# A recurrent and FP4 feed-forward layer on one core: stacking the short Down slice, splitting the pointwise product, moving layernorm sums and reordering the first chunk

## The reference

```
xn = layernorm(x)
# branch s: causal conv -> recurrence -> MLP, each with an RMS norm and a residual
x1 = pointwise(causal_dwconv3(rmsnorm(xn))) + xn
x2 = scan(sigmoid(gate), g(hidden)) + x1        # gate, hidden = rmsnorm(x1) @ gru_w.T
s  = gelu(rmsnorm(x2) @ w1.T + b1) @ w2.T + b2 + x2
# branch g: a SwiGLU whose operands are rounded to FP4 in blocks of 16
h  = silu(fp4(xn) @ fp4(w_gate).T) * (fp4(xn) @ fp4(w_up).T)      # 704 wide
g  = silu(fp4(h) @ fp4(w_down).T)
out = x + s * g
```

## Time and profile before

| | us |
|---|---|
| median of 3 runs (1084.41 to 1086.84) | 1085.59 |
| the profiled execution | 1085.26 |
| its span, first to last instruction | 1083.5 |
| PE busy in the span | 1061.8 (98%) |
| DVE busy | 934.5 (86%) |
| ACT busy | 607.3 (56%) |
| POOL busy | 147.5 (14%) |

### The profile page before, as it was taken

How to read it: one execution, slowest core, us unless ns; L and a number is a source line. 1 busy time by engine, 2 the same in 40 slices (tenths; PEclk the granted TensorE clock), 3 DMA queues, 4 the chain that set the end, 5 groups by cost and what they waited for, 6 DMA issues and landing times. The chain is left out here.

```text
span 1083.5 us, 18319 instructions
## 1 busy us (share of the span) xinstructions
PE 1061.8 (98%) x6954; PEld 967.9 (89%) x6954; DVE 934.5 (86%) x1720; ACT 607.3 (56%) x967; POOL 147.5 (14%) x123
## 2 busy tenths in 40 slices
PE   7899999999999999999999999999999999999998
PEld 6788989989898998989999898998989899898998
DVE  6978988989888898988889898898989889898895
ACT  5564464564746547474654747455574645647452
POOL 1230101112020110201111010111101011120010
PEclk9999999999999999999999999999999999999999
DMA  7000001010010101001010010101001010100110
GB/s 248 1 21 1 1 2 59 1 60 1 1 59 1 59 1 47 13 2 59 1 60 1 21 40 1 59 1 60 1 1 59 1 59 1 59 1 2 39 40 21
DMA packets 29365, 31.45 MB, mean 29 GB/s; under 512 B 1120, under 2 KB 28512, under 8 KB 29280
## 3 DMA queue, kind: packets, MB, share of 16 engines
q1 hardware_dynamic: 28448, 29.43, 8.7%
q10 hardware_dynamic: 832, 0.87, 0.2%
HBM read 21.90 MB, written 8.39 MB: 28 GB/s over the span
## 5 line engine op out<-in xcount | busy, mean ns | idle before, releaser
L990 PE MATMUL gu_ps<-gu_hi,xq_hi 128*128 128x352 f32 x512 | 168.3, 329 | 0.0
L990 PE MATMUL gu_ps<-gu_lo,xq_hi 128*128 128x352 f32 x512 | 165.9, 324 | 0.0
L990 PE MATMUL gu_ps<-gu_hi,xq_lo 128*128 128x352 f32 x512 | 165.7, 324 | 0.0
L990 PE MATMUL w_ps<-w_hi,act_hi 128*128 128x256 f32 x480 | 140.1, 292 | 0.0
L990 PE MATMUL w_ps<-w_hi,act_lo 128*128 128x256 f32 x480 | 135.1, 281 | 0.0
L990 PE MATMUL w_ps<-w_lo,act_hi 128*128 128x256 f32 x480 | 134.9, 281 | 0.0
L990 PE MATMUL w_ps<-dn_hi,hqt_hi 128*128 128x256 f32 x384 | 116.6, 304 | 2.0 <-DVE hqt_lo L519 2.0
L990 PE MATMUL w_ps<-dn_hi,hqt_lo 128*128 128x256 f32 x384 | 108.5, 283 | 0.0
L990 PE MATMUL w_ps<-dn_lo,hqt_hi 128*128 128x256 f32 x384 | 108.4, 282 | 0.0
L818 ACT ACTIVATE g<-w_ps 128x256 f32<-128x256 f32 x64 | 24.7, 385 | 147.7 <-PE w_ps L990 147.6
L496 DVE TENSOR_TENSOR hid<-sl,gu_ps 128x704 f32<-128x704 f32 x64 | 56.8, 887 | 58.8 <-PE gu_ps L990 58.2
(11 more groups left out here) (136 smaller groups left out, 2703.6 us busy)
## 6 DMA issues: line engine op xcount, KB each, us to landing
x_in<-x_dram SPq DMA_DIRECT2D x16, 512.0 KB, 5.8
x_res<-x_dram SPq DMA_DIRECT2D x16, 512.0 KB, 5.0
out_dram<-o SPq DMA_DIRECT2D x15, 512.0 KB, 3.5
act<-w_t_dram SPq DMA_DIRECT2D x1, 1024.0 KB, 11.3
w_f<-w_t_dram SPq DMA_DIRECT2D x1, 1024.0 KB, 13.8
w_f<-w_down_dram SPq DMA_DIRECT2D x1, 704.0 KB, 9.4
hid<-w_gate_dram SPq DMA_DIRECT2D x1, 640.0 KB, 5.9
hid<-w_up_dram SPq DMA_DIRECT2D x1, 640.0 KB, 9.3
```

The source lines that it names most:

```text
L990: done = M.matmul(psum, l, r, start=first and i == 0, stop=last and i == len(terms) - 1)
```

## The change

- Down: `fp4_hidden_values` writes the last 64 quantised features twice, so the sixth slice holds them in rows 0 to 63 and again in rows 64 to 127 (the memset is gone). `hidden_low` makes low parts for five slices in one subtraction and, in a second small one, replaces rows 64 to 127 of the sixth high slice by their low part. `down` then needs 5 x 3 + 2 = 17 matmuls for a tile.
- Pointwise: `pw` and `y` are split in high and low parts. PE does three fp32r matmuls in place of each fp32 product (12 in place of 8 instructions for a chunk); ACT gets `front_y_high`, DVE `front_y_low`. `y_hi` and `y_lo` share their memory with `keep` and `cand`.
- Layernorm sums: `front_moments` is cut in two. `front_stats(c+2)` is the last DVE step of `body(c)`, and the rest (aggregation) moves into the next body between `hidden_values(c-1,2)` and the second group of `gelus_low`. SP issues each `load` ahead of the `store` beside it.
- `gelus_low` is cut as `range(4)` and `range(4, 8)` in place of `range(5)` and `range(5, 8)`. `output_sum` is as before.
- Small moves in `body`: `output(c-1,1)` ahead of `scaled_low(2c+1)`, `front_xc(c+1)` ahead of all of `ff1(c)`, `front_y` behind the first gelu, the taps ahead of the last quantisation step.
- `first()`: the low parts of `w1` and `w2` are made on DVE (`ff_low`) and no longer on POOL, and the weight steps 3 to 5 go between the tiles of `ff1(0)`; some `keep_busy` counts change; `pointwise(1)` is last.

The core of the diff:

```diff
             with sp.Fori(0, B - 3) as i:
+                load(i + 3)
                 store(i)
-                load(i + 3)
...
             def first():
                 layernorm_scales(0, 1)
-                low_weights(0)
+                gru_low()
                 rms_scale(0)
-                pool.wait_ge(xslo_ready, KD)
-                low_weights(1)
                 rms_scale(1)
-                pool.wait_ge(xslo_ready, 2 * KD)
-                low_weights(2)
                 layernorm_scales(1, 3)
...
+            def fp4_hidden_values(dst, rounded):
+
+                n, last = NBI * FP4_BLOCK, NFULL * P // FP4_BLOCK
+                fp4_values(dst[:, 0:n], NBI, rounded)
+                return V.scalar_tensor_tensor(blocks(dst[:, n:KI * P], NBI - last),
+                                              blocks(q_m[:, NFULL * P:n].bitcast(BF16), NBI - last),
+                                              1.0 / UNIT, spread(q_scale[:, last:NBI], NBI - last),
+                                              ALU.mult, ALU.mult)
...
-                V.tensor_tensor(hqt_lo[:], hqt_ps, hqt_hi[:].bitcast(F32), ALU.subtract).then_inc(hqtlo_ready, 1)
+                V.tensor_tensor(hqt_lo[:], hqt_ps[:, 0:NFULL, :], hqt_hi[:, 0:NFULL, :].bitcast(F32), ALU.subtract)
+
+                twin = hqt_hi[LAST:P, NFULL, :]
+                V.tensor_tensor(twin, hqt_ps[LAST:P, NFULL, :], twin.bitcast(F32),
+                                ALU.subtract).then_inc(hqtlo_ready, 1)
...
             def body(c, front):
                 hidden_values(c - 1, 1, fp4_round(NBI, carried["ratios"]))
-                gelus_low(c - 1, range(5))
+                gelus_low(c - 1, range(4))
                 hidden(c, 0)
...
                 hidden_values(c - 1, 2, fp4_round(NBI, ratios))
-                gelus_low(c - 1, range(5, KF))
+                if front and c > 1:
+                    front_moments(carried["stats"])
+                gelus_low(c - 1, range(4, KF))
                 hidden(c, 2)
...
-                if front:
-                    front_moments(c + 1)
+                if front and c == 1:
+                    front_moments(front_stats(c + 1))
                 recurrence(c, 0)
...
+                output(c - 1, 1, w_ps[:, 1, :])
                 scaled_low(c * 2 + 1)
-                output(c - 1, 1, w_ps[:, 1, :])
...
                 if front:
-                    front_fp4_values(c + 1, front_fp4_ratios(c + 1))
+                    ratios = front_fp4_ratios(c + 1)
                     front_taps(c + 1)
+                    front_fp4_values(c + 1, fp4_round(T * NBD, ratios))
+                    front_y_low(c + 1)
                     carried["ratios"] = fp4_ratios(hid[:, 1, :], NBI, hidden_scales(c, 1))
                     hidden_low(c, 0)
                     front_fp4_low(c + 1)
+                    if c + 2 < B:
+                        carried["stats"] = front_stats(c + 2)
...
-                        last = product(w_ps[:, e, :], pw[:, k, e * P:(e + 1) * P], y[:, k, :], False, k == KD - 1)
+                        last = product(w_ps[:, e, :], (pw_hi[:, k, e * P:(e + 1) * P], pw_lo[:, k, e * P:(e + 1) * P]),
+                                       (y_hi[:, k, :], y_lo[:, k, :]), False, k == KD - 1)
...
-                for k in range(KI):
-                    last = product(bank[:, 0:D], (hqt_hi[:, k, :], hqt_lo[:, k, :]),
-                                   (dn_hi[:, k, :], dn_lo[:, k, :]), k == 0, k == KI - 1)
-                last.then_inc(dn_done, 1)
+                for k in range(NFULL):
+                    product(bank[:, 0:D], (hqt_hi[:, k, :], hqt_lo[:, k, :]), (dn_hi[:, k, :], dn_lo[:, k, :]),
+                            k == 0, False)
+
+                M.matmul(bank[:, 0:D], hqt_hi[:, NFULL, :], dn_lo[:, NFULL, :], start=False, stop=False)
+                M.matmul(bank[:, 0:D], hqt_hi[:, NFULL, :], dn_hi[:, NFULL, :], start=False,
+                         stop=True).then_inc(dn_done, 1)
```

More of the change, by code:

```diff
@@ L439, in front_moments @@
                     last = V.bn_stats(stats[:, t, :], x_in[:, t, :])
-                s = steps.mark(last)
+                return steps.mark(last)
+            def front_moments(s):
                 dve.wait_ge(dve_step, s)
@@ L757, in front_y, with front_y_high @@
                                  scale=dww[:, k, 2:3]).then_inc(y0_ready, 1)
+            def front_y_high(c):
+                for k in range(KD):
+                    act.wait_ge(y_ready, KD * c + k + 1)
+                    act.wait_ge(pw_done, KD * c)
+                    act.wait_ge(x2_ready, KD * c)
+                    A.copy(y_hi[:, k, :], y[:, k, :]).then_inc(yhi_ready, 1)
             def front_xq(c):
@@ L889, in first @@
                 high_weights(0)
+                front_y_high(0)
                 front_xq(0)
@@ L953, in body @@
                 biased_residual(c)
-                for j in range(KF // 2):
+                gelus(c, (0,))
+                if front:
+                    front_y(c + 1)
+                gelus_high(c, (0,))
+                for j in range(1, KF // 2):
                     gelus(c, (j,))
@@ L1146, in weight_rest @@
                 for i, (hi, bank) in enumerate(places):
-                    last = M.matmul(bank, minus_ident[:], hi, start=False, stop=i == len(places) - 1)
+                    last = M.matmul(bank, minus_ident, hi, start=False, stop=i == len(places) - 1)
                 last.then_inc(wqm_done, 1)
@@ L1173, in down_rest @@
                     n = min(4, KI - k)
-                    last = M.matmul(hqt_ps[:, k:k + n, :], minus_ident[:], dn_hi[:, k:k + n, e * P:(e + 1) * P],
+                    last = M.matmul(hqt_ps[:, k:k + n, :], minus_ident, dn_hi[:, k:k + n, e * P:(e + 1) * P],
                                     start=False, stop=True)
@@ L1203, in first @@
                 weight_rest(2)
+                keep_busy(24, w_ps[:, 0, :])
+                sum_squares(1, gu_ps[:, 0, 0, :], (coef_ready, 1))
+                keep_busy(8, w_ps[:, 0, :])
+                spread_scale(1, gu_ps[:, 0, 1, :], (cand_ready, 1))
                 weight(3)
-                weight_rest(3)
-                keep_busy(20, w_ps[:, 0, :])
-                sum_squares(1, gu_ps[:, 0, 0, :], (coef_ready, 1))
-                weight(4)
-                keep_busy(7, w_ps[:, 0, :])
-                spread_scale(1, gu_ps[:, 0, 1, :], (cand_ready, 1))
-                weight_rest(4)
-                weight(5)
                 keep_busy(8, w_ps[:, 0, :])
                 pe.wait_ge(whi_ready, 2 * KD)
-                pe.wait_ge(wlo_ready, 2 * KD)
-                ff1(0, range(1))
+                pe.wait_ge(flo_ready, KD)
+                ff1(0, (0, 1))
+                weight_rest(3)
+                ff1(0, (2,))
+                weight(4)
+                ff1(0, (3,))
+                weight_rest(4)
+                ff1(0, (4,))
+                weight(5)
+                ff1(0, (5,))
                 weight_rest(5)
-                ff1(0, range(1, KF // 2))
+                ff1(0, (6, 7))
                 down_weight(0)
-                ff1(0, range(KF // 2, KF))
-                down_rest(0)
                 pe.wait_ge(wqlo_ready, NFULL + 1)
                 gate_up(0, 0, 0)
-                down_weight(1)
+                down_rest(0)
                 gate_up(0, 0, 1)
                 gate_up(0, 1, 0)
+                down_weight(1)
+                gate_up(0, 1, 1)
                 down_rest(1)
-                gate_up(0, 1, 1)
                 front_xc(1)
@@ L1263, in body @@
                 ff2(c - 1, 2, w_ps[:, 2, :], (g_ready, T * c))
-                ff1(c, range(KF // 2))
                 if front:
@@ L1267, in body @@
                     front_xc(c + 1)
+                ff1(c, range(KF // 2))
+                if front:
                     ff1(c, range(KF // 2, KF))
```

180 lines of the change are left out of this document (107 added, 73 removed).

## The result

The changed kernel takes 1144.96 us (median of 4 runs, 1144.2 to 1146.28), the kernel before 1085.0 beside it: a ratio of 1.0551, with a 95% interval of 1.0533 to 1.057. The forecast was 1146, 5.6% slower.

The account below looks back on a forecast made before the run. PE, busy 98% of the span, was taken to bound the kernel. Span 1083.5 - 4.0 - 9.1 + 55.0 + 23.8 - 5.5 + 0.4 = 1144.1, plus 1.8 and 0.3: 1146 us; range 1119 to 1166.

Parts of the forecast that it names:

- Down: down on PE: 17 matmuls in place of 18, 0.119 us each, gaining in 34 of 64 calls: -4.0 us.
- Pointwise: Pointwise product on PE: 12 split matmuls in place of 8 fp32 instructions, 0.65 us saved in 14 bodies: -9.1 us.
- The new DVE work at nothing: Added DVE steps, about 2.2 us a chunk, taken as covered by 8 us of DVE idle time: no cost.
- The stall: First spread_scale of bodies 2 to 15: PE waits 3.97 us for POOL's scale, queued behind output_sum: +55.0 us.
- E: Start of sum_squares on PE in a body, from which the prediction counted; scale forecast 10.30 us later.
- The clock: PE behind each long wait at the first spread_scale: a fall to the lower clock, 14 x 1.7: +23.8 us.
- The rival without a fall: PE behind the waits at the first spread_scale: clock stays up, 1122 us; chance 0.15.
- The first chunk: Work ahead of the bodies: filled gru wait, fewer POOL low parts, earlier ff1(0): -5.5 us, bounds -8 and +2.
- The tail: End of the run: DVE's chain to the last low parts grows by three small writes: +0.4 us.
- The faster rival: First spread_scale: POOL's chain ends before PE gets there, so only savings are left: 1066 us; chance 0.05.

Follow-up runs that it names:

- the run with the guard moved: The changed kernel with output_sum waiting for the fourth subtraction of gelus_low in place of the fifth: 1092.59 us, 1.0071 of before.
- filled run: The changed kernel with 16 idle products on PE ahead of the first spread_scale in bodies 2 to 15: 1124.01 us, 1.0363 of before.
- the run with the groups alone: The kernel before with only the groups of gelus_low cut at four in place of five: 1149.51 us, 1.06 of before.
- the run with groups and sums back: The changed kernel with gelus_low groups of five and three and all of front_moments in its old place: 1081.94 us, 0.9966 of before.

## Why the prediction was right, and where it was not

**Down.** 17 matmuls at 0.12 us hold. Which calls gain was right for the changed kernel: the wait at the second `spread_scale` grew by what `down(c-1,3)` lost.

**Pointwise.** In the run with the guard moved the product and its transposes take 3.69 us a chunk, against 4.31 before: 0.62 saved, forecast 0.65.

**The new DVE work at nothing** was right only by accident. I took 2.2 us of additions against 8 us of idle time in a chunk. That was the wrong comparison: idle time is where DVE waits for others, and the additions lie elsewhere. The stack's share cost 0.7% by itself. In the changed kernel the stall of 3.8 us covered it, which the prediction did not say; this part of the forecast came out by luck. The second small subtraction was also mis-sized: 0.29 us net for the pair, not 0.1.

**The stall.** 3.97 us were forecast; from where PE was due (584.82 + 6.33) to 594.97 it is 3.82. The parts erred in opposite ways: POOL's sum was marked as started 6.00 us behind E and took 2.67 for 2.40, so it was through 0.26 us sooner than I had it, and the scale took 1.46 us for 1.23. That POOL gets in behind the sixth subtraction, not the eighth, is what the row of the seventh shows (2.83 us).

**The clock.** Forecast 1.7 us for each fall. From `spread_scale` to the next `down` it is 6.58 us (594.97 to 601.55) against 4.95 before (1014.85 to 1019.80): 1.63. The `down` in the changed kernel, then before:

```profile
601.55 0.28 PE L1061 MATMUL w_ps<-dn_hi,hqt_hi 128*128 128x256 f32 x1
```

```profile
1019.80 2.14 PE w_ps L990 x18
```

The filled run gives 1.5 for the whole. The rival without a fall, 1122, is what that run measured (1124): the price was right, and the condition was not met.

**The first chunk** is the term that was mis-sized. Forecast -5.5; body 1 starts at 101.63 in place of 103.39, and a fall of the clock of which 0.7 us lay behind that point is gone: -2.5. About half of that may be the clock and not the new order: in the run with the groups alone, whose first chunk is that of the kernel before, the same two waits (1.96 and 1.97 us) had no fall behind them, and the first `sum_squares` of body 1 started at 111.45 in place of 112.54. Two things were left out: `pw_lo` goes in front of `xn` on DVE, and POOL's low parts of `gru_w` stretch two DVE operations, by 1.8 us together:

```profile
9.39 0.69 DVE L650 TENSOR_TENSOR pw_lo<-w_f,pw_hi 128x512 fp32r<-128x512 f32 x1 [1.17 <-ACT pw_hi L946]
10.00 1.38 DVE L467 TENSOR_SCALAR xn<-x_in,moments,rstd 128x256 f32<-128x256 f32 x4
...
18.92 1.91 DVE L428 SCALAR_TENSOR_TENSOR xq<-q_e,q_scale 128x1024 f32<-128x1024 bf16 x1
...
20.75 2.36 DVE L501 TENSOR_TENSOR y_lo<-cand,y_hi 128x512 fp32r<-128x512 f32 x2
```

Before, DVE waited there too, for POOL's `rstd`:

```profile
9.15 1.38 DVE L459 TENSOR_SCALAR xn<-x_in,moments,rstd 128x256 f32<-128x256 f32 x4 [1.21 <-POOL rstd L337]
```

So the wait of 1.17 us for `pw_hi` mostly takes the place of an old one. With the 0.3 us taken off by which the whole run starts later (first load 5.55 for 5.26), `xn` comes 0.6 us later.

**The tail**: forecast +0.4. The wait of 1.74 us became 2.33, and behind it the clock fell: 24 matmuls and two transposes took 4.6 us (1120.02 to 1124.63) where they took 3.1: +2.1 in all. The prediction had the row that says 1.74 us was short of a fall and didn't ask what 0.5 more would do. The answer is not the same each time. The 5 us behind this wait, in the changed kernel and, behind 2.30 us, in the run with groups and sums back:

```profile
1120.02:1125.02 5.00, 5.00 (x30) 5.00 (x31) 4.71 (x10) 0.20 (x1) 0.00 (x0) 0.66 0.00 0
```

```profile
1056.27:1061.27 5.00, 5.00 (x42) 5.00 (x43) 4.71 (x10) 0.23 (x1) 0.00 (x0) 1.00 0.00 0
```

So 0.6 us of the 2.1 are the longer wait, and 1.5 a fall of the clock that such a wait brings in one run and not in another.

**The faster rival** was put at 1066, on the ground that without the POOL chain only savings are left. With the guard moved it was 1092.6. Its condition was right and its price wrong, by the step "new DVE work at nothing" and by the moved layernorm sums, which it gave no price: of the 26 us between the two, 10.6 came back with groups and sums in their old places, and 11.5 with `bn_stats` out of the chain ahead of `add_squares`.

In sum, with the measured terms: 1083.5 - 4.0 - 9.1 + 53 + 23 - 2.5 + 2.1 = 1146, beside a span of 1144.5; with the 21 us of the filled run for the clock it is 1144. The mechanism and its two large terms were right. That the total is right within 1 us is luck: the errors at the ends (4.7 us too low) and in the stall with the clock (3 to 5 us too high) cancelled.

## What to carry to other kernels

When a step is moved across a count that some guard uses, look up every waiter on that count and what is queued behind the waiter: here one subtraction moved from the first group to the second put 3 us into each of 14 chunks (3.8 with the steps that were added in front of it), by way of a third engine. Cost new work on an engine along the chain on which it lies, not against the engine's idle time in a chunk; 0.4 us on the chain that ends last outweighed 8 us of idle elsewhere. And when a stall is removed, expect the one that it covered: here three limits lay beneath one another, and only with all three seen to did the savings show (1070 us).

## What the hardware showed

- Behind the start, every wait of PE of 2.86 us or more in these traces was followed by its lower clock (all 30), and none of 1.86 us or less was. In between it differs: of the 17 waits of 1.96 to 2.33 us nine were followed by it and eight were not, the same wait of the same step (1.96 us ahead of the gru, 2.30 in the tail) now one way and now the other. A fall cost 1.5 to 1.65 us; one, in the run with the groups alone, cost about 3 (a chunk of 69.99 us among chunks of 68.6). Idle products in the wait prevented it (14 of 14).
- A POOL sum that reads 1024 columns from two tensors and DVE subtractions with two SBUF inputs didn't overlap: DVE's four took 4.64 us for 2.49, POOL's one 2.67 for 2.40. POOL did not have to wait for a gap in DVE's list: it got in between the second and the third of four back-to-back subtractions.
- The Trainium skill ("SBUF — State Buffer", "Who interferes with whom") says that such a pair contends for a port that the two share, and that it is an exclusive lock. The trace agrees, and shows the lock taken for one instruction, not for a row of them.
